# Value rows of the attention loaded per pair of tiles, and seven late weight loads moved, in a one-core transformer kernel

## Time and profile before

| | |
|---|---|
| median of three runs | 738.68 us (736.33 to 741.09) |
| the profiled execution | 743.06 us |
| its span, first to last instruction | 741.3 us |
| mean granted TensorE clock | 0.909 |
| busy over the span: PE, PEld, DVE, ACT, POOL | 547.0, 459.0, 590.3, 350.8, 456.8 us |
| moved by DMA | 64.79 MB |

### The profile page before, as it was taken

The page is one execution under the profiler, slowest core; times in us unless marked ns, Lnnn a source line. Parts: engine busy times, 40 slices in busy tenths (PEclk is TensorE's granted clock), DMA queues, the critical chain, the costliest instruction groups (busy, mean ns, idle before and its releaser), DMA issues.

```text
span 741.3 us, 42186 instructions
## 1 busy us (share of the span) xinstructions
PE 547.0 (74%) x17799; PEld 459.0 (62%) x17799; DVE 590.3 (80%) x1860; ACT 350.8 (47%) x549; POOL 456.8 (62%) x623
## 2 busy tenths in 40 slices
PE   0445978887999678877365788777887778877776
PEld 0344867776887446646344677666776677766665
DVE  5534766785888569998578888999999999999982
ACT  4333555564667334655314344455544455544540
POOL 7523434453463234646217778898888888889981
PEclk9978898997999889999566799999999999999997
DMA  6684485777571101000001213222232322223211
GB/s 217 189 232 114 126 235 131 172 229 205 152 182 33 44 1 29 16 28 0 4 6 39 64 47 70 69 70 52 62 71 64 71 52 62 71 64 71 67 46 38
DMA packets 45574, 64.79 MB, mean 87 GB/s; under 512 B 5712, under 2 KB 37712, under 8 KB 42960
## 3 DMA queue, kind: packets, MB, share of 16 engines
q1 hardware_dynamic: 45520, 64.04, 33.7%
HBM read 36.49 MB, written 8.65 MB: 61 GB/s over the span
## 4 chain that ended last, share of the span: by engine, by line
DVE 39%; PE 36%; issue 18%; POOL 3%; DMA 1%; DVEq 1%; ACT 1%; SPq 0%; POOLq 0%; ACTq 0%
PE ps L745 9%; DVE top L1312 6%; PE ps L760 6%; PE ps L909 5%; PE ps L725 5%; DVE prod L1367 4%; DVE tile_rows L1149 4%; DVE wq_sb L1343 4%; PE ps L735 3%; PE ps L888 3%; DVE best L1323 3%; DVE r_x L1352 2%; DVE stats L1129 2%; DVE hid L1358 2%; PE ps L771 2%
## 5 line engine op out<-in xcount | busy, mean ns | idle before, releaser
L909 PE MATMUL ps<-up_sb,prod 128*128 128x128 f32 x512 | 80.4, 320 | 48.1 <-DVE prod L1367 47.9
L930 ACT ACTIVATE arena<-ps 128x512 f32<-128x512 f32 x128 | 70.5, 595 | 94.9 <-PE ps L745 94.8
L909 PEld LDWEIGHTS ps<-up_sb,prod 128*128 128x128 f32 x512 | 74.1, 227 | 54.5 <-DVE prod L1367 54.5
L888 PE MATMUL ps<-arena,hid 128*32 128x32 f32 x8192 | 81.5, 200 | 22.2 <-issue 18.3
L888 PEld LDWEIGHTS ps<-arena,hid 128*32 128x32 f32 x8192 | 76.8, 113 | 27.2 <-issue 19.4
L1093 DVE TENSOR_REDUCE row_max<-ps 128x8 f32<-128x768 f32 x64 | 61.0, 953 | 28.2 <-PE ps L735 27.5
L660 POOL TENSOR_TENSOR wq_sb<-wq_sb,tile_rows 128x1024 f32<-128x1024 f32 x32 | 76.3, 2385 | 9.3 <-POOL tile_rows L656 8.5
L745 PE MATMUL ps<-ident,arena 128*128 128x128 f32 x512 | 75.0, 295 | 1.9 <-issue 1.6
L1039 ACT ACTIVATE out_tile<-ps,shift,rstd 128x128 f32<-128x128 f32 x32 | 14.6, 458 | 121.3 <-POOL shift L684 121.3
L897 PEld LDWEIGHTS ps<-xT,downT_sb 128*128 128x128 f32 x512 | 64.3, 197 | 12.0 <-issue 11.0
L745 PEld LDWEIGHTS ps<-ident,arena 128*128 128x128 f32 x512 | 66.3, 155 | 3.8 <-issue 1.3
(11 more groups left out here) (157 smaller groups left out, 1336.8 us busy)
## 6 DMA issues: line engine op xcount, KB each, us to landing
arena<-r_x SPq DMA_DIRECT2D x128, 128.0 KB, 2.4
early<-terms SPq DMA_DIRECT2D x16, 360.0 KB
xT<-terms SPq DMA_DIRECT2D x16, 360.0 KB
hid<-terms SPq DMA_DIRECT2D x16, 360.0 KB
prod<-terms SPq DMA_DIRECT2D x16, 360.0 KB
x_tile<-in_x_wrapped SPq DMA_DIRECT2D x32, 128.0 KB, 6.6
x<-in_x SPq DMA_DIRECT2D x8, 256.0 KB, 2.7
xT_tile<-xT SPq DMA_DIRECT2D x32, 64.0 KB, 1.9
```

Of the source, the lines that this page charges most:

```text
L888: mm = nc.tensor.matmul(slots[32 * g:32 * g + 32, k, c], leftT[p][:, r // 2, r % 2, :], blocks_of[p][:, :, r // 2, r % 2, GROUP * g:GROUP ...
L909: mm = nc.tensor.matmul(ps[:, 6 + p, 0:P], pairs[:, c // 2, c % 2], up_sb[:, c, :], start=False, stop=(c == EC - 1))
L930: return nc.scalar.activation(out_ap, in_ap, ACT.Copy)
```

## The change

The two `x_tile` buffers (two slabs each, one tile) become two `x_pair` buffers (four slabs each, the edge and mid slabs of a pair of tiles). One load, `x_load(j, u)`, brings 256 KB for the pair j. It waits until the mid copies of pair j-2 are done. The loads of pairs 0 and 1 move behind rows(0) and behind rows(1); for i = 1 there is none; for later i the load of pair i follows rows(i+1). The last load (the edge slab of tile 32) waits for one mid copy less. `x1_b2` uses the same memory as `x_pair`.

Eight weights (layer-norm rows, b2, b1, w1, w2) are still loaded at i = 5 to 8. The other seven (w_q, w_qT, keysT, gamma, beta, downT, up) are issued after the first two loads of the feed-forward stage, and raise a semaphore of their own, `late_in`, on which TensorE waits before the products with `second_moment` and VectorE after writing it. The waits before the feed-forward stage are for eight weights.

```diff
-        x_tile = two("x_tile", [P, 2, P])
+        x_pair = two("x_pair", [P, 4, P])
...
-        x1_b2 = two("x1_b2", [P, 4, P])
+        x1_b2 = x_pair
...
+        late_in = sem("late_in")
...
-        N_WEIGHTS = 15
+        N_WEIGHTS = 8
+        N_LATE = 7
...
-            def x_load(t, p, n=2):
-
-                need(sp, mid_ready, t - 1)
-                at = x_wrapped[bass.ds(t * P, P), :]
-                sp.dma_start(x_tile[p][:, 0:n], bass.AP(at.tensor, at.offset, [[P, P], [2 * W * P, n], [1, P]])
-                             ).then_inc(x_in[p], 16)
+            def x_load(j, u, n=4):
+
+                need(sp, mid_ready, 2 * (j - 1))
+                at = x_wrapped[bass.ds(2 * j * P, P), :]
+                sp.dma_start(x_pair[u][:, 0:n], bass.AP(at.tensor, at.offset, [[P, P], [2 * W * P, n], [1, P]])
+                             ).then_inc(x_in[u], 16)
...
                 if i == 0:
-                    for p in range(2):
-                        x_load(p, p)
                     keep_terms(0)
                     sp.wait_ge(rows_cleared, 4)
                     sp.wait_ge(terms_out[0], 64)
                     rows(0)
+                    x_load(0, 0)
                     rows(1)
+                    x_load(1, 1)
                     keep_terms(1)
                     continue
...
-                x_load(2 * i, 0)
-                x_load(2 * i + 1, 1)
+                if i > 1:
+                    x_load(i, i % 2)
                 if i in (1, 3, 4):
                     keep_terms(2 + i // 2)
                 if i >= 5:
-                    for dst, src in itertools.islice(weights, 2):
+                    for dst, src in itertools.islice(weights, 0 if i >= 9 else 2):
                         sp.dma_start(dst, src).then_inc(weights_in, 16)
-            x_load(NT, 0, 1)
+            x_load(PAIRS, 0, 1)
...
+                if first:
+                    for dst, src in weights:
+                        sp.dma_start(dst, src).then_inc(late_in, 16)
             over_pairs(sp, NQ // 2, b2_loads)
...
-            def edge_values(t, i, p):
-
-                pool.wait_ge(x_in[p], 16 * (i + 1))
+            def edge_values(t, j, k):
+
+                p, u = k % 2, (k // 2) % 2
+                if p == 0:
+                    pool.wait_ge(x_in[u], 16 * (j + 1 + k // 4))
                 need(pool, pv_done, GROUPS * (t - 1))
                 hold(pool)
-                nc.gpsimd.tensor_copy(v_edge[p][:, :, 0:DH], heads_of(x_tile[p][:, 0])).then_inc(edge_ready, 1)
+                nc.gpsimd.tensor_copy(v_edge[p][:, :, 0:DH], heads_of(x_pair[u][:, 2 * p])).then_inc(edge_ready, 1)
...
-                nc.gpsimd.tensor_copy(v_mid[p][:, :, 0:DH], heads_of(x_tile[p][:, 1])).then_inc(mid_ready, 1)
+                nc.gpsimd.tensor_copy(v_mid[p][:, :, 0:DH], heads_of(x_pair[u][:, 2 * p + 1])).then_inc(mid_ready, 1)
...
+            pe.wait_ge(late_in, 16 * N_LATE)
             pe.wait_ge(moment_ready, 1)
...
+            v.wait_ge(late_in, 16 * N_LATE)
```

More of the change, by code:

```diff
@@ L519, in heads_of, with mid_values @@
                 return flat.rearrange("p (h d) -> p h d", d=DH)
-            def edge_values(t, i, p):
-                pool.wait_ge(x_in[p], 16 * (i + 1))
+            def edge_values(t, j, k):
+                p, u = k % 2, (k // 2) % 2
+                if p == 0:
+                    pool.wait_ge(x_in[u], 16 * (j + 1 + k // 4))
                 need(pool, pv_done, GROUPS * (t - 1))
                 hold(pool)
-                nc.gpsimd.tensor_copy(v_edge[p][:, :, 0:DH], heads_of(x_tile[p][:, 0])).then_inc(edge_ready, 1)
-            def mid_values(t, p):
+                nc.gpsimd.tensor_copy(v_edge[p][:, :, 0:DH], heads_of(x_pair[u][:, 2 * p])).then_inc(edge_ready, 1)
+            def mid_values(t, k):
+                p, u = k % 2, (k // 2) % 2
                 pool.wait_ge(edge_ready, t + 1)
@@ L547, in b1_operands @@
                 for k in range(4):
-                    t, i, p = 4 * j + k, 2 * j + k // 2, k % 2
-                    edge_values(t + 1, i + p, 1 - p)
+                    t = 4 * j + k
+                    edge_values(t + 1, j, k + 1)
                     if not (last and k > 0):
@@ L552, in b1_operands @@
                     if not (last and k == 3):
-                        mid_values(t + 1, 1 - p)
+                        mid_values(t + 1, k + 1)
             copy_rows(0, 0, 0)
```

## The result

| | before | after |
|---|---|---|
| median of 20 runs each | 739.62 us (732.94 to 746.24) | 731.79 us (725.04 to 737.98) |
| ratio of after to before, 95% interval | | 0.9885 (0.9858 to 0.9912) |
| the profiled execution, its span | 743.06, 741.3 us | 727.66, 725.9 us |
| mean granted TensorE clock | 0.909 | 0.917 |

The change saves about 1.1%, 8 us. Medians are over all executions; ratios leave out those more than 1.5% above the kernel's fastest. The two profiled executions differ by twice the medians' 8 us, 15.4 us.

The account below looks back on a forecast made before the run. It took TensorE's stops at edge copies, whose loads land behind rows on q1, as open to this change. Terms 4 + 12.9 - 2 gave 15 us off the 738.7 us median: 723.7 us, its own range 716 to 731.

Parts of the forecast that it names:

- The steady part: Attention stage, edge copies 12 to 30: period per pair falls from 12.13 to 10.7 us, 12.9 us gained over nine pairs.
- the rule: Attention stage: a late load delays every second pair, so a pair's period is (L + 7.5) / 2, 10.5 to 10.85 us.
- L: Attention stage: time from T to the landing of the load, 14.4 us before, forecast 13.5 to 14.2 us.
- T: Attention stage: end of GpSimd's row copy of tile 2j-1, which releases the rows of pair j+1.
- The opening: Attention stage up to edge copy 12: 4 us gained, between -2 and 8, mainly from tile 8's earlier load.
- The late weights: End of attention stage: moved weights lengthen TensorE's code stop near 243 us, 2 us lost, bounds 0 and 9.
- the first rival: Attention stage: loads stay nearly as late, period 11.4 us, 8.6 us gained, 730 us; chance 0.17.
- The fourth rival: Attention stage: rows and loads keep the 16 DMA engines full, L passes 17 us, 11 us lost, 749 us; chance 0.05.
- The second: Rival for the attention stage: no edge copy waits and the weights cost nothing, 19.6 us gained, 719 us; chance 0.15.
- The rule beside it: Attention-stage transfers: about 2 us plus bytes over 436 GB/s; rows and pair load down 5.9 us after issue, 15.6 us gained.

Follow-up runs that it names:

- the later session: The changed kernel timed again without edit, beside the kernel before: 729.78 against 741.99 us, ratio 0.983.
- pairs only: Changed kernel with all 15 weights loaded in the attention stage again, so pair loads alone: 735.15 against 744.74 us of the kernel before, ratio 0.9885.
- late only: Kernel before with only the seven weights moved behind the first loads of the feed-forward stage: 740.46 us, ratio 0.996.
- the later weights: Changed kernel, load of pair i ahead of rows(i+1), seven weights after the last feed-forward loads: 722.53 us, 0.974 of before; 717.91 us in another session.

## Why the prediction was right or wrong

**The steady part held in the first trace, and in the second less.** Forecast: 10.7 us a pair, 12.9 us gained. Measured: 10.70 and, in the second trace, (219.28 - 118.35) / 9 = 11.2, against 12.13 and 12.3, so 11.5 us gained in the mean. For tile 28 the rule, half of L plus 7.5 us, held in its parts: L 13.8 us (13.5 to 14.2 forecast), and 216.01 + 1.47 - 209.99 = 7.5 us of recovery. But the sum set a rule tried on two good pairs (11.07) against a mean of nine (12.13). By the rule alone 14.4 us of L before against 13.8 are 0.3 us a pair. The rest came from pairs on which the rule was not tried. Before, up to tile 20, GpSimd took 8.9 to 9.9 us from a late edge copy to the end of the row copy two pairs on, and after, 7.4 to 8.1 in the first trace; what shortened it no run singles out. And tile 20, behind 2 MB of weights, had its load landing 19.8 us after T before; its copy starts 14.3 us after T now. The prediction has 18.0 there, with tile 28's lag of 5.7 us between T and issue; tile 20's was 7.5 us (T 159.7, issue 167.25). That the total came out near is in part luck.

**The opening held, by its stated cause.** 4 us forecast at edge copy 12; 125.1 and 125.6 became 121.5 and 118.4, 5.4 us, with up to 3 us between executions of one code. Tile 8's load came 13.8 us after T (82.5 to 96.3), and tile 10's was held behind 8 term transfers that took SP 10.45 us to issue. I had that copy at 111 to 112 us; it came at 112.3.

**The late weights held as a stop.** 2 us forecast: the stop went from 2.0 to 3.9 and 4.0 us in two traces each. What moving them out of the attention stage buys was in the steady part's sum without a size of its own: 4.3 us at edge copy 32 on top of the pair loads, 7 to 9 us by itself in the steady part.

**Where it was wrong.** The sum was 15 us and the stage gave 15.6, yet the medians moved 7.8 us in 20 runs each and 12.2 in the later session. The 731.8 us lie closer to the first rival's 730 than to 723.7, though its period of 11.4 us is in neither trace of the changed kernel. The step that failed is "the gain lies in waits that every run has, so I take 15 off the median". It took a stage's gain for the kernel's.

Behind edge copy 32 the traces take from 489 to 497 us in six runs whose code there is the same but for the weights' loads and the waits for them: 494.4, 489.2 and 491.8 without late weights (before twice, pairs only), 494.2, 494.7 and 497.2 with them (the changed kernel twice, late only). The granted clock over this whole part goes with it, 0.92 for the 489.2 and 491.8 us and 0.91 for the other four; that of the product-key stage's first 90 us alone does not, with 0.98 in the trace of 494.7. Two traces of each kernel say 494.5 after and 491.8 before for that part, 2.7 us given back, and with 15.6 - 2.7 = 13 us the traced executions agree (741.7 against 728.7 us in the mean).

Two explanations stay open: late weights that cost something behind edge copy 32 too, against which stand the two traces with the load ahead of the rows, 490.1 us with the same late weights; or a part that differs by 8 us between executions whatever the change, of which two traces each caught these. The difference from the medians is 5 us for the first session and 1 for the later; whether it lies in the attention stage of the untraced executions or behind it, no run here separates.

**Its own signs.** It said it would be wrong if the opening's code stops changed by more than 2 us in all, if waits for rows took the place of those for value rows, or if the part after 250 us moved. The two long stops changed by 0.5 us in sum, but with the shorter ones between 36 and 80 us they fell from 17.7 to 14.1 us. GpSimd's wait for rows in the opening did take the place of one for value rows. And the last part moved, between executions of the same kernel first of all. Of what should show, the waits of even edge copies stayed under 2 us in only three of eight: from tile 14 to 28 they are 0.9 to 3.5 us. The clock from 125 to 200 us was 1.00 in the first trace, as forecast, and 0.95 in the second.

The fourth rival fell with L. The second did not come, because the load stayed behind the rows; moved ahead of them it came at once. The rule beside it in the prediction, from "DMA: Bandwidth & Descriptors" in the Trainium skill (section on the anatomy of one DMA), was measured on transfers that GpSimd issues; SP's 1.7 MB here took 13.8 us from T, not 5.9.

## What to carry to other kernels

A load that lands late behind a bulk transfer on the same queue was cured here by its place, not by its size: the double buffer paid most when it was used to issue the small, urgent load ahead of the bulk one (23 to 27 us) and less when the load stayed behind (8 to 12 us), both with the late weights. And bulk transfers that nobody needs yet delay the urgent ones wherever they stand in front of them: moving them alone took 7 to 9 us out of the steady part. Sum a stage's gain from the engine that sets its end, not from the waits of its helper, whose total says little here, and do not take a stage's gain for the kernel's when the other stages differ by 8 us between executions. And before a 1% change is judged, run the same kernel against itself.

## What the runs showed of the hardware

- TensorE stops for code while data fills the DMA engines. On the first pass of its loop the longest such stop was 5.8 to 7.2 us in the twelve traces with full rows, and 1.7 us with a tenth of the bytes. At the end of the attention stage it was 3.7 to 4.8 us in the seven traces with late weights under way and 1.3 to 2.0 in the six without. The code queue moves one packet there in both kernels, while q1 takes 97.5% of the engines in the changed one (225.5 to 231 us) and 12.8% before (242 to 247 us).
- The same code of the product-key stage was given a clock of 0.89 to 1.00 in the same 90 us of different executions and kernels, and did 2345 to 2625 matmuls in them.
- A 256 KB load landed 3.2 us after issue ahead of 1.4 MB of rows, and 10.6 us after issue, 13.8 us after the rows' release, behind them.
- How far executions of one kernel spread did not follow from how little TensorE stops in the attention stage: 712 to 723 us in 12 runs with the load ahead of the rows, but 714 to 731 in 12 with the later weights as well, and 737 to 753 in 17 of the kernel before.
